# Expert result rows added to token rows in memory, two accumulators, plain loads in place of the gathers

## The reference, cut to what matters

```python
hg = jnp.einsum('ecd,efd->ecf', expert_in, w_gate)
hu = jnp.einsum('ecd,efd->ecf', expert_in, w_up)
expert_out = jnp.einsum('ecf,edf->ecd', jax.nn.silu(hg) * hu, w_down)
...
sparse = jax.ops.segment_sum(fg[:, None] * expert_out.reshape(-1, D), dst, num_segments=N + 1)[:N]
return shared_out + sparse.reshape(B, S, D)
```

## Time and profile before

| | us |
|---|---|
| median of 3 runs | 2253.76 (2252.62 to 2260.72) |
| the profiled execution | 2264.58 |
| its span | 2262.9 |
| PE busy in the span | 1961.3 (87%) |
| POOL busy in the span | 642.9 (28%) |
| DMA packets | 121600, 282.58 MB |

### The profile page before, as it was taken

One profiled execution on the slowest core, in us unless ns is written; L12 is line 12 of the kernel. 1 busy time (PEld: TensorE's weight loads), 2 busy tenths in 40 slices (PEclk: granted clock), 3 DMA queues, 4 the chain that ended last, 5 costly groups with the idle time before them and its releaser, 6 DMA issues. The chain is left out here.

```text
span 2262.9 us, 36818 instructions
## 1 busy us (share of the span) xinstructions
PE 1961.3 (87%) x10769; PEld 1500.4 (66%) x10769; DVE 1354.7 (60%) x1930; ACT 1112.2 (49%) x1779; POOL 642.9 (28%) x470
## 2 busy tenths in 40 slices
PE   5875996979789999999877679999999966999998
PEld 2554443445377777777665368888668845899997
DVE  6773877253258667767501444555343259999996
ACT  2663663220057667667501046666332227767674
POOL 3001000007635334444274077677100004000000
PEclk8997998979999999999989889999999988999999
DMA  2203931113168779878465166777211040000001
GB/s 87 77 14 67 371 64 51 56 39 96 41 223 307 256 241 331 300 265 287 155 164 152 46 171 185 186 190 190 64 33 38 28 167 1 1 1 1 0 0 46
DMA packets 121600, 282.58 MB, mean 125 GB/s; under 512 B 51616, under 2 KB 58778, under 8 KB 111966
## 3 DMA queue, kind: packets, MB, share of 16 engines
q1 hardware_dynamic: 53646, 189.25, 24.6%
q0 software_dynamic: 67792, 91.34, 14.1%
HBM read 242.05 MB, written 53.89 MB: 131 GB/s over the span
## 5 line engine op out<-in xcount | busy, mean ns | idle before, releaser
L2059 PE MATMUL ps<-ft,kw 128*128 128x125 f32 x2880 | 343.6, 280 | 36.0 <-DVE ft L1984 22.9
L2059 PEld LDWEIGHTS ps<-ft,kw 128*128 128x128 f32 x2880 | 331.7, 194 | 50.0 <-DVE ft L1984 29.3
L1143 POOL DMA_INDIRECT xg<-nrows,idx x128 | 211.0, 1649 | 273.6 <-PE ps L1169 244.0
L1461 POOL DMA_INDIRECT pg<-prows,srcI x170 | 209.7, 1233 | 83.6 <-issue 44.1
L1492 PE MATMUL ps<-ehot,msg 125*128 125x125 f32 x1360 | 164.8, 280 | 20.8 <-ACT ehot L1584 15.8
L1492 PEld LDWEIGHTS ps<-ehot,msg 125*128 125x128 f32 x1360 | 158.9, 195 | 35.0 <-issue 26.6
L2008 ACT ACTIVATE ksq<-ksrc,kn 128x750 f32<-128x750 f32 (+2 forms) x144 | 116.7, 814 | 97.2 <-DVE cube L1967 97.2
L1182 PE MATMUL ps<-wh,xh 128*128 128x512 f32 x364 | 152.0, 418 | 6.3 <-DVE xl L1300 5.1
L1928 POOL COPY ksrc<-nT 128x500 f32<-128x500 f32 (+1 forms) x10 | 10.8, 1075 | 490.2 <-SPq L1919 250.8
L1287 DVE TENSOR_TENSOR wgl<-wexp,wh 128x2048 fp32r<-128x2048 f32 x64 | 146.6, 2291 | 0.3 <-issue 0.3
L1227 ACT ACTIVATE wh<-wexp 128x2048 fp32r<-128x2048 f32 x64 | 122.6, 1918 | 45.2 <-PEq L824 44.4
(11 more groups left out here) (296 smaller groups left out, 4267.5 us busy)
## 6 DMA issues: line engine op xcount, KB each, us to landing
wexp<-wexp_d SPq DMA_DIRECT2D x64, 1024.0 KB
wexp<-wexp_d SPq DMA_DIRECT2D x64, 512.0 KB
yrows<-y SPq DMA_DIRECT2D x91, 256.0 KB
yrows<-nought POOLq DMA_DIRECT2D x1, 16384.0 KB, 56.1
attr<-attr_d SPq DMA_DIRECT2D x42, 250.0 KB
kw<-kw_d SPq DMA_DIRECT2D x2, 4608.0 KB
qs<-qk SPq DMA_DIRECT2D x32, 156.2 KB, 6.7
ks<-qk SPq DMA_DIRECT2D x32, 156.2 KB, 7.0
```

The costliest lines, as they stand in the source:

```text
L1143: pool.indirect_dma_start(xg[:, e % 2, h, :], None, d["nrows"], bass.IndirectOffsetOnAxis(ap=idx[:, 2 * e + h:2 * e + h + 1], axis=0), bou ...
L1461: pool.indirect_dma_start(pg[:, p % 4, t % 2, :], None, d["prows"], bass.IndirectOffsetOnAxis(ap=c.srcI[:, t:t + 1], axis=0)).then_inc(s_g ...
L2059: mm = pe.matmul(out[:, m * B:m * B + B], w[:, k, f, m * P:m * P + P], ft[:, f % RF, a:a + B], start=False, stop=False, skip_group_check=True)
```

## The change

The table `yrows` (16384 rows) is replaced by two accumulators `arows0` and `arows1` of AR = 1408 rows each. Both are filled with zeros in the attention stage. After each step, POOL adds the 128 rows of `y` into the accumulator of the expert's parity (e % 2), row by row at the token's number, with an indirect transfer that adds. Blank slots point at rows N + partition, a separate one for each partition. Two transfers of the same accumulator never run together: POOL waits for the last one of that parity. The combination loads the two accumulators with 20 plain transfers from SP and sums two blocks in place of six.

```diff
@@ attention, POOL
-                second = d["yrows"][0:DUMP, :].rearrange("(p e h) f -> p e h f", p=P, h=2)[:, :, 1, :]
-                pool.dma_start(second, nought ... broadcast_to([P, NE, D])).then_inc(s_rows, 16)
-                pool.wait_ge(s_rows, 16)
+                for q in range(2):
+                    pool.dma_start(d[f"arows{q}"].rearrange("(p r) f -> p r f", p=P),
+                                   nought ... broadcast_to([P, AR // P, D])).then_inc(s_rows, 16)
+                pool.wait_ge(s_rows, 32)
@@ routing, POOL (and the row of zeros at yrows[DUMP] is gone)
-                pool.memset(blank[:, :, 0], float(N))
+                pool.iota(blank[:, :, 0], pattern=[[0, CH]], base=N, channel_multiplier=1, ...)
@@ experts
-        y = sb("y", [CH, 2, 2, D], F32)
+        y = sb("y", [CH, 2, D], F32)
+        pick = sb("pick", [CH, 2], U32)
@@ experts, SP: the stores of y and ylast are gone, the loads of the weights stay
-                        sp.wait_ge(s_y, n + k + 2)
-                        to = sp.snap(col, min_val=0, max_val=P - 1)
-                        sp.dma_start(ydst[:, bass.ds(to, 1), :], y[:, e % 2, bass.ds(k, 1), :])\
-                            .then_inc(s_st[e % 2], 16)
+                for e in range(WR, NE):
+                    sp.wait_ge(s_glo, e - WR + 1)
+                    load(e, GU, s_rgu)
+                    sp.wait_ge(s_dlo, e - WR + 1)
+                    load(e, DN, s_rdn)
@@ experts, POOL
+                def scatter(q, source, n, done):
+                    column = bass.ds(pool.snap(col, min_val=0, max_val=P - 1), 1)
+                    picked, there = pool.snap(n + 1), pool.snap(n + 2)
+                    pool.wait_ge(s_st[q], done)
+                    pool.sem_inc(s_mark, 1)
+                    pool.tensor_copy(pick[:, q:q + 1], idx[:, column]).then_inc(s_pick, 1)
+                    pool.wait_ge(s_pick, picked)
+                    pool.wait_ge(s_y, there)
+                    pool.sem_inc(s_mark, 1)
+                    pool.indirect_dma_start(
+                        d[f"arows{q}"], bass.IndirectOffsetOnAxis(ap=pick[:, q:q + 1], axis=0), source, None,
+                        bounds_check=AR - 1, oob_is_err=True, compute_op=ALU.add).then_inc(s_st[q], 16)
                 for e in range(NE):
+                    q = e % 2
                     pool.wait_ge(s_t, e + 1)
                     if e + 2 < NE:
                         gather(e + 2)
+                    n, m = pas.sum("pooln", e, 2 * e), pas.sum(f"pool{q}", e // 2, e // 2 * 2)
+                    with pool.Fori(0, pas.count(e)) as k:
+                        scatter(q, y[:, q, :], n + k, pool.snap((m + k + 1) * 16))
+                        pool.reg_mov(col, pool.to_reg(k + 2 * e))
+                    pas.add("pooln", e)
+                    pas.add(f"pool{q}", e)
+                    pas.fetch(e + 1)
+                ...
+                scatter(0, ylast[:, :], pas.sum("pooln", NE, 2 * NE), ends[0])
@@ experts, ACT: hh before y, and the wait for the buffer moved into the step
-                    if e >= 2:
-                        act.wait_ge(s_st[q], pas.sum(f"act{q}", e // 2, e // 2 * 2) * 16)
-                        act.wait_ge(s_dn, n + k + 1)
-                        act.activation(y[:, q, bass.ds(k, 1), :].rearrange("p o f -> p (o f)"), c.ps[:, DOWN, :],
-                                       ACT.Copy).then_inc(s_y, 1)
                         act.wait_ge(s_th, n + k + 1)
                         act.activation(hh[:, :, :].rearrange("p k n -> p (k n)"), c.psf[:, TURN:TURN + 2 * CH], ACT.Copy)\
                             .then_inc(s_hh, 1)
+                        act.wait_ge(s_dn, down_done)
+                        act.wait_ge(s_st[q], free)
+                        act.activation(y[:, q, :], c.ps[:, DOWN, :], ACT.Copy).then_inc(s_y, 1)
@@ combination
-            @block.gpsimd  (60 indirect gathers from yrows)
+            @block.sync
+            def _(sp):
                 for b in range(NB):
+                    for q in range(2):
+                        sp.dma_start(part[:, b, q, :], d[f"arows{q}"][b * B:b * B + B, :]).then_inc(s_p[b], 16)
@@ combination, PE: "for k in range(TOPK)" becomes "for q in range(2)"
```

More of the change, by code:

```diff
@@ L52 @@
 DUMP = P * CH
+AR = -(-(N + CH) // P) * P
 _WIDTHS = [("bq", 2), ("bk", 2), ("ba", KD), ("bf", KD), ("b2", KD), ("bih", 12), ("bhh", 12), ("gamma", KD),
@@ L815, in routing @@
         ones16 = sb("ones16", [B, B], F16)
-        zero = sb("zero", [1, D], F32)
-        blank = sb("blank", [P, CH + 1, 2], F32)
+        blank = sb("blank", [P, CH, 2], F32)
         cnt, pre, unit = (sb("x" + n, [1, NE], F32) for n in ("cnt", "pre", "unit"))
@@ L827, in _ @@
                 sp.wait_ge(s_zero, 1)
-                sp.dma_start(d["slots"].rearrange("(p r) t -> p (r t)", p=P), blank[:, :, :].rearrange("p r t -> p (r t)"))\
-                    .then_inc(s_init, 16)
-                sp.dma_start(d["yrows"][DUMP:DUMP + 1, :], zero[0:1, 0:D]).then_inc(s_init, 16)
+                sp.dma_start(d["slots"][0:DUMP, :].rearrange("(p r) t -> p (r t)", p=P),
+                             blank[:, :, :].rearrange("p r t -> p (r t)")).then_inc(s_init, 16)
                 for b in range(NB):
@@ L838, in _ @@
                     sp.wait_ge(s_rs[i], 16 * len(range(i, NB, RS)))
-                sp.wait_ge(s_init, 32)
+                sp.wait_ge(s_init, 16)
             @block.gpsimd
             def _(pool):
-                pool.memset(zero[:, :], 0.0)
-                pool.memset(blank[:, :, 0], float(N))
+                pool.iota(blank[:, :, 0], pattern=[[0, CH]], base=N, channel_multiplier=1,
+                          allow_small_or_imprecise_dtypes=True)
                 pool.memset(blank[:, :, 1], 0.0).then_inc(s_zero, 1)
@@ L1151, in _ @@
                 gather(1)
+                for q in range(2):
+                    pool.dma_start(d[f"arows{q}"][AR - 1:AR, 0:1], c.one[0:1, :]).then_inc(s_st[q], 16)
+                pas = Passage(c, pool, "pool")
+                for name in ("pooln", "pool0", "pool1"):
+                    pas.total(name)
+                col = pool.alloc_register("ycol")
+                pool.reg_mov(col, 1)
+                def scatter(q, source, n, done):
[10 more added lines that the diff above has]
+                        bounds_check=AR - 1, oob_is_err=True, compute_op=ALU.add).then_inc(s_st[q], 16)
                 for e in range(NE):
+                    q = e % 2
                     pool.wait_ge(s_t, e + 1)
@@ L1155, in _ @@
                         gather(e + 2)
+                    n, m = pas.sum("pooln", e, 2 * e), pas.sum(f"pool{q}", e // 2, e // 2 * 2)
[5 more added lines that the diff above has]
+                    pas.fetch(e + 1)
+                ends = [pool.snap((pas.sum(f"pool{q}", NE // 2, NE) + 1) * 16) for q in range(2)]
+                last = pool.snap(ends[0] + 16)
+                scatter(0, ylast[:, :], pas.sum("pooln", NE, 2 * NE), ends[0])
+                pool.wait_ge(s_st[1], ends[1])
+                pool.wait_ge(s_st[0], last)
             @block.tensor
@@ L1328, in _ @@
                     pas.add("dven", e)
[L1331 removed]
     with ExitStack() as ctx:
[L1333 to L1334 removed]
+        part = ctx.enter_context(nc.sbuf_tensor("part", [B, NB, 2, D], F32))
+        s_p = [c.sem(f"co_p{b}") for b in range(NB)]
         s_sum, s_x = c.sem("co_sum"), c.sem("co_x")
         with nc.Block() as block:
[L1337 to L1338 removed]
+            @block.sync
+            def _(sp):
                 for b in range(NB):
[L1340 to L1345 removed]
+                    for q in range(2):
+                        sp.dma_start(part[:, b, q, :], d[f"arows{q}"][b * B:b * B + B, :]).then_inc(s_p[b], 16)
             @block.tensor
@@ L1351, in _ @@
                         pe.wait_ge(s_x, b - 1)
-                    for k in range(TOPK):
-                        pe.wait_ge(s_p[b % PS][k], 16 * (b // PS + 1))
+                    pe.wait_ge(s_p[b], 32)
+                    for q in range(2):
                         for m in range(KD):
-                            mm = pe.matmul(c.ps[:, b % 2, m * B:m * B + B], part[:, b % PS, k, m * P:m * P + P],
-                                           c.ident[0:B, 0:B], start=(k == 0 and m == 0), stop=(k == TOPK - 1),
+                            mm = pe.matmul(c.ps[:, b % 2, m * B:m * B + B], part[:, b, q, m * P:m * P + P],
+                                           c.ident[0:B, 0:B], start=(q == 0 and m == 0), stop=(q == 1),
                                            skip_group_check=True)
```

56 lines of the change are left out of this document (8 added, 48 removed).

## The result

The changed kernel takes 2452.14 us (median of 4 runs, 2446.16 to 2462.62) against 2256.41 us for the kernel before in 4 runs beside it: a ratio of 1.087 [1.083, 1.091], slower by 196 us. I had forecast 2325 in a range of 2235 to 2440, slower by 72.

What follows compares the result with a forecast made beforehand. PE was taken to bound the experts, POOL's gather issue the combination. The profiled 2264.58 + 147 (order of POOL's list) - 75 (combination) = 2337 us; the median lies 10.8 lower, so 2325 was said, range 2235 to 2440.

Steps and rivals of the forecast that it cites:

- third rival: Experts: adding is slow in the DMA engines, G 15.35 to 16.5, +237 to +274 us, kernel 2415 to 2453; 20%.
- G: Experts: time from R to the landing of gather(e+3), forecast 12.45 us; above 5.4 a following one-step expert is late.
- The order of POOL's list: Experts: gather(e+3) now follows the add of expert e, so PE waits at its turns: +147 us.
- R: Experts: the moment PE is ready for the turn at the end of expert e.
- The second wait, on ACT: Two-step experts: second y waits some 2 us for the first add's landing, 27 times, covered before Silu: 0.
- The experts' own lengths: Experts: time between turns kept at the old pace, 5.4 us for one step and 10.3 for two.
- The combination, -75: Combination: 20 plain loads at 373 GB/s replace 60 gathers, 27 us in place of 102: -75 us.
- a rate under 300 GB/s: Combination: sign that the prediction is wrong, if its loads don't reach 300 GB/s.
- Adding issue as a plain scatter: POOL's issue of an adding transfer, when free, taken to last as long as a plain scatter's: 1.2 us.
- What goes at no gain: Smaller zero fill, 91 stores off SP, blank table by iota, hh before y: 0, at most 0.9 us from the fill.
- gathers land early: Experts: landing of 2.0 to 3.0 us, stage +33 to +54 us, kernel 2212 to 2233; 12%.

Runs made afterwards that it cites:

- gather_first: Changed kernel with POOL issuing the gather of expert e+3 ahead of the adds of expert e: 2317.14 us, ratio 1.034 to the kernel before.
- order_alone: Changed kernel with no adding transfer issued, all waits and pick copies kept in order: 2317.53 us, ratio 1.033 to the kernel before.
- plain_write: Changed kernel with each add made a plain indirect write of the same rows: 2375.47 us, ratio 1.059 to the kernel before.
- load128: Changed kernel with the combination's 20 loads taking 128 rows in place of 125: 2411.84 us, ratio 1.078 to the kernel before.
- short_low: Changed kernel with DVE's two weight subtractions cut to 128 columns: 2400.69 us, ratio 1.058 to the kernel before.
- gather_first_load128: Changed kernel with gathers ahead of the adds and combination loads of 128 rows: 2322.42 us, ratio 1.0235 to the kernel before.
- crossed_if: gather_first_load128 with an expert's second add to the other accumulator, a y slot per step, pick copy before the gather: 2315.76 us, ratio 1.021.
- gather_first_no_add: gather_first with the adding transfers left out, all waits kept: 2196.58 us, ratio 0.968 to the kernel before.

## Why the prediction was wrong

The direction was right, the size was not: +196 instead of +72. 2452 lies at the upper end of the third rival (2415 to 2453), but by another way: that rival had it all in G, through the gathers' landing, and G was 13.3.

- *The order of POOL's list, G.* Right, and nearly right in size: +147 forecast, +161 measured. For the 20 one-step experts behind which PE waited, the means are: the add started at R + 2.5 (I had 1.6), took 2.55 (2.65), the gap was 0.3 (0.9), the gathers took 2.9 (2.3) and the landing 5.0 (5.0): G = 13.3 against 12.45. In 15 of them the add started at R + 1.8 to 2.0, as it came 0.9 us after `y` had ended (1168.19 to 1169.10 above) where I allowed 0.4; in five, behind an expert that was itself late, at R + 4.1 to 4.2. One of the two gathers was sometimes held by DVE. Behind two-step experts (18 cases) the add started at R + 4.7, as it is the second of two and waits for the landing of the first, which my steps of G left out. As the add was mostly free of DVE's pair there (1.7 us) and the gathers landed in 4.2, G was 13.8. gather_first and order_alone each show the order by itself.
- *"The second wait, on ACT: covered, 0".* This step failed. I let Silu be ACT's next work after `y`, some 4 us later. In ACT's list the roundings of weights for later experts stand between them (1.05 + 1.91 us), so ACT has no such gap. The wait is 56 us in the trace, and 28 of them reach PE, as idle time in the intervals that follow a two-step expert. With the adding taken out (plain_write) ACT's wait is 21 us and PE's extra idle time is gone.
- *The experts' own lengths, taken as unchanged.* This step failed by more: some 52 of the 80 us are PE's own busy time for the same products (511 in place of 458 in all). It follows PE's idle time and not the adds: with no adds at all (order_alone, where nobody waits for a landing) the lengths are still 31 us longer (36 x 0.61 + 25 x 0.37), all of it busy time. What follows a long idle time of PE is slow: the turn behind the wait of 10.22 us takes 1.97 instead of 1.08 us, at a granted clock of 0.50, and in the changed kernel one-step lengths after a wait of more than 3.9 us average 7.63 against 6.78 over all. The mean granted clock between the turns is 0.86 in the changed kernel, 0.89 in plain_write and 0.91 in order_alone, against 0.99 before, and the waits for gathers are 175, 144, 104 and 13. A wait of PE cost more than its own length, and my sum had it at exactly its length.
- *The combination, -75.* Measured -40. The direction was right. The mis-sized term is the loads at 373 GB/s: the row behind it, the zero fill of the earlier trace rows, is of transfers of another shape, and I should have asked for a row of 125 partitions or bounded it by one. That is 29 of the 35 us (48.3 instead of 19), and a rate under 300 GB/s was one of the prediction's own signs of being wrong. The other 6 stand ahead of the loads, 13.7 us where I had 7.7: POOL's DRAIN of 7.25 us (1.35 in the kernel before) where I had 1.5 of barrier, 1.2 until the add starts and 0.4 more for its issue, less a landing of 3.3 instead of 5.
- *Adding issue as a plain scatter, 1.2 us.* It is 1.57 to 1.64. The 0.4 us is small where POOL waits; it counts where POOL is the bound, as in the stretch of gather_first above.
- *What goes at no gain.* The stores and the zero fill: nothing in the rows contradicts it.
- *Rivals.* That gathers land early is refuted by the landing of 5.0. The DMA engines do spend more on an add (26.9% against 14.1%), but in one-step experts G kept a landing of 5.0; the adding reached the time through the landing waits of ACT and POOL, the latter inside G of the two-step experts. Between plain_write and the changed kernel the waits for gathers differ by 31 us, PE's idle time inside by 29 and its busy time by 13.

## What to carry to other kernels

Before giving an in-order engine a wait for a late result, look at what else is behind that wait in its list, and issue first whatever another engine needs soonest: here that alone was 5% of the kernel. To call a wait covered, write down the engine's whole list between the waiting instruction and the next one that somebody needs, prefetch work for later experts included; and if the wait reaches TensorE, expect to pay its length and a slower clock after it. A read-add-write chain in memory is only as fast as its landings, and a rate taken from one transfer may not hold for another of other shape: here 128 rows against 125 made 313 GB/s of 121.

## What the runs showed of the hardware

- An adding indirect transfer of 128 rows of 2 KB took POOL 1.57 to 1.64 us to issue when DVE's weight pair didn't hold it, a plain one 0.99 to 1.07. In the changed kernel it landed 3.3 us (median) after the end of its issue when POOL issued nothing behind it, and 6.1 us when a gather followed; plain writes 1.8 and 5.4. The DMA engines' time of that queue was 26.9% with adding and 14.1% with plain writes.
- POOL's queue DRAIN at the end of the experts' block came after the last transfer had landed. It took 7.25 to 7.33 us in five kernels with adds (the changed one, load128, short_low, gather_first, gather_first_load128), 4.23 in crossed_if, 9.13 after plain indirect writes, and 1.35 and 1.37 us where POOL issues only gathers in that block (the kernel before, order_alone, gather_first_no_add). What sets its length is open.
- Plain loads of 125 rows ran at 121 GB/s with 0.32 of the DMA engines busy, and SP's issue of one took 0.28 to 0.34 us for the first four and 1.83 (median of 20) once more were under way. Loads of 128 rows ran at 313 GB/s with 0.43 us to issue one.
- An instruction of POOL that depends on a copy just ahead of it on POOL started 0.98 us after the copy's end (44.2 us in 45 waits).
- Behind a wait of 10.22 us PE ran at a granted clock of 0.50, and 5 us later at 1.00.
